# Reordering the last items of a fused token-mixing, attention and int8 kernel, and moving one item to the folded right side

## The chip, the cores and the metric

The kernel runs on one core of a Trainium2 chip. Its time is the device time in microseconds (us) of one execution; the profile's span is the part of it between the first and the last recorded instruction.

## The reference

Four batch rows of 512 image tokens are mixed from `x`, 77 text tokens are appended to each, and two residual blocks follow:

```python
h = einsum('bhid,oi,od->bho', x, weighted_sum, weight)      # 4 x 512 x 256
h = concatenate([h, txt], axis=1)                           # 4 x 589 x 256
h = h + attn(layernorm(h))     # gate * U * cumsum(V) @ out_w + 3-tap convolution along the tokens
n = layernorm(h)
lhs_scale = absmax(n, per row) / 127;   rhs_scale = absmax(rhs, per column) / 127
h = h + (round(n / lhs_scale) @ round(rhs / rhs_scale)) * lhs_scale * rhs_scale
```

## The kernel before

**Tiling.** The tokens of the image are worked in eight *groups* of 256 (two per batch row). The second half of the work goes by twelve *items*, three per batch row: items 0, 3, 6, 9 and 1, 4, 7, 10 are the two blocks of 256 image tokens, items 2, 5, 8, 11 the 77 text tokens. A block of 256 tokens lies as two tiles of 128 partitions by 256 columns, so most steps on it are two instructions and those on a text item are one.

**Stages of an item.** PE adds the convolution (`local`, L1000) and the gated product (`mix`, L1021) to the item's PSUM bank. DVE takes the statistics (`stats`, L717 and L720). POOL works out the reciprocal root (`rstd`, L409). ACT centres the rows (`centre`, L645) and copies them as the residual (`keep`, L653). DVE takes the maximum of each row and its reciprocal (`scale`, L828 and L830). POOL rounds to int16 (`round`, L484) and works out the row's scale (`lscale`, L476). PE transposes (`q_turn`, L1041), ACT turns the integers back into numbers (`ints`, L629), PE multiplies by the right side (`ffn`, L1062 or L1067), DVE scales the product (`out`, L863 or L853), and SP stores the result (L388).

**Two forms of the last steps.** For items below `FIN_ON_DVE` the right side is bf16 integers (`qrhs`, L1062: four matmuls for an item of 256 tokens). DVE then writes the scaled product to `tmp` (L863), and POOL adds the residual into `fin` (L496). For the items from `FIN_ON_DVE` on, the right side has its column scales folded in and is split into two fp32r parts (`srhs_high` of L535, `srhs_low` of L781; L1067: eight matmuls for 256 tokens, four for a text item), and DVE adds the residual itself, into `fin` (L853). The copy of the integers (L629) goes to `qT` in one case and to `qT_wide` in the other.

**Two accumulators.** From item 7 (`ACC_TWO`) on, the products alternate between `uvg_ps` (items 7, 9, 11) and `acc_ps` (items 8, 10). A product waits until the output of the item two before it has been read (L1053 to L1057): product 8 for item 6's output, product 9 for item 7's, product 10 for item 8's, product 11 for item 9's.

**What sets the order.** Each engine runs its own list in strict order. The lists are written out by hand as places: `GROUP_AT` and `ITEM_AT` (L27, L55) give each stage of each group or item a number, and every engine steps through the places and issues what is due. At one place a fixed order of stages holds. For the end of the program the lists before are:

- PE: transpose 8 (1032), convolution 11, product 7 (1034), mix 11 (1035), transpose 9 (1036), product 8 (1037), seven filler matmuls (`WARM_AT`, 1038), transpose 10 (1039), product 9 (1040), product 10 (1041), transpose 11 (1042), product 11 (1043).
- DVE: statistics 10 (73), output 6 (74), scale 10 (75), output 7 (76), statistics 11 (77), output 8 (78), scale 11 (79), outputs 9, 10, 11 (80 to 82).
- POOL: rounding 10 (66), add 7 (67), rounding 11 (68), row scale 10 (69), reciprocal root 11 (70), row scale 11 (71), with the add of item 6 (65) ahead of them.
- ACT: copy 8 (95), keep 8, centre 10 (97), keep 9 (98), copy 9 (99), keep 10 (100), centre 11 (101), copy 10 (102), copy 11 (103), keep 11 (104).

The fillers (`keep_warm`, L1072) multiply a tile of ones into `xt_ps`, which nothing reads afterwards. Another four stand at the start of the program (L1077).

Of the kernel before, what the change touches and what calls it, by code (L numbers as in the profile page):

```python
# [5 lines left out]
P = 128  # L6
# [21 lines left out]
    stats=(2, 6, 13, 23, 31, 40, 50, 57),  # L28
    rstd=(0, 4, 8, 15, 21, 32, 41, 44),
# [26 lines left out]
    put=(-1, -1, 33, -1, -1, 57, -1, -1, 82, -1, -1, 94),  # L56
    conv=(449, 450, 593, 721, 723, 817, 1011, 1015, 1021, 1026, 1028, 1033),
    mix=(451, 465, 594, 722, 724, 818, 1012, 1016, 1024, 1027, 1030, 1035),
    stats=(20, 21, 29, 38, 39, 45, 58, 63, 65, 69, 73, 77),
    rstd=(12, 27, 29, 31, 36, 37, 48, 51, 56, 58, 64, 70),  # L60
    centre=(28, 30, 39, 52, 54, 62, 77, 86, 90, 91, 97, 101),
    keep=(29, 31, 40, 53, 55, 65, 81, 92, 96, 98, 100, 104),
    scale=(24, 25, 34, 42, 43, 48, 61, 66, 70, 72, 75, 79),
    round=(16, 17, 25, 34, 39, 46, 49, 54, 61, 62, 66, 68),
    lscale=(19, 28, 38, 43, 45, 53, 57, 59, 60, 63, 69, 71),
    turn=(609, 641, 753, 898, 1010, 1018, 1025, 1029, 1032, 1036, 1039, 1042),
    ints=(41, 51, 64, 70, 74, 80, 87, 93, 95, 99, 102, 103),
    product=(643, 754, 945, 1013, 1019, 1022, 1031, 1034, 1037, 1040, 1041, 1043),
    out=(33, 41, 53, 59, 62, 68, 74, 76, 78, 80, 81, 82),
    fin=(24, 33, 42, 47, 50, 55, 65, 67),  # L70
)

TXT_AT = dict(turn=337, hidden=354, gates=369, stats=4, uv=12, norm=10, move=13, relu=16, sigmoid=18, rstd=2)
RHS_AT = dict(turn=370, low=0, round=11, out=14, fold=22, fold_low=55, high=0, fold_high=63)
DIAG_AT = 3
WARM_AT = {1038: 7}

FIN_ON_DVE = 8
ACC_TWO = 7
PLAIN = 1  # L80
BY_DMA = 3
# [5 lines left out]
def early_fusion_kernel(nc, x0, x, ws, wt, txt, par, rhs, out, B, HI, T, D, ND, GH, R):  # L87
# [8 lines left out]
    GROUPS = B * HALVES  # L96
# [15 lines left out]
    def item(j):  # L112
        b, i = divmod(j, ITEMS_PER_B)
        return b, i, (2 if i < HALVES else 1), (P if i < HALVES else T)
# [7 lines left out]
    def groups(place, stage):  # L122
        return [g for g, at in enumerate(GROUP_AT[stage]) if at == place]

    def items(place, stage):
        return [j for j, at in enumerate(ITEM_AT[stage]) if at == place]
# [6 lines left out]
    with ExitStack() as ctx:  # L133
        def sb(name, shape, dt=F32):
            return ctx.enter_context(nc.sbuf_tensor(name, shape, dt))

        def sem(name):
            return ctx.enter_context(nc.semaphore(name))
# [50 lines left out]
        lscale = sb("lscale", [P, ITEMS, 2])  # L189
# [6 lines left out]
        fin = sb("fin", [P, 4, 2, D])  # L196
# [14 lines left out]
        def bank(name):  # L211
            return ctx.enter_context(nc.psum_tensor(name, [P, 512], F32))

        h_ps = [bank(f"h_ps{n}") for n in range(4)]
        xt_ps = bank("xt_ps")
# [22 lines left out]
        def wait_fin(eng, j):  # L238

            if j < FIN_ON_DVE:  # L240
                eng.wait_ge(fin_pool, j + 1)
            else:
                eng.wait_ge(fin_dve, j - FIN_ON_DVE + 1)

# [81 lines left out]
        xnT_ready = sem("xnT_ready")  # L326
# [67 lines left out]
        def _(pool):  # L394
# [53 lines left out]
            for place in range(PLACES):  # L448
# [40 lines left out]
                for j in items(place, "fin"):  # L489
                    if j < FIN_ON_DVE:  # L490
                        _, _, nt, rows = item(j)
# [9 lines left out]
        def _(act):  # L501
# [91 lines left out]
            for place in range(PLACES):  # L593
# [29 lines left out]
                for j in items(place, "ints"):  # L623
                    _, _, nt, rows = item(j)
                    act.wait_ge(qt_done, j + 1)
                    if j >= 2:
                        act.wait_ge(acc_done, j - 1)
                    dst = qT if j < FIN_ON_DVE else qT_wide
                    nc.scalar.activation(dst[:, j % 2, :, 0:nt * rows], q16_v[:, :, 0:nt * rows].bitcast(I16),  # L629
# [55 lines left out]
        def _(dve):  # L685
# [117 lines left out]
            for place in range(PLACES):  # L803
# [41 lines left out]
                for j in items(place, "out"):  # L845
                    _, _, nt, rows = item(j)
                    dve.wait_ge(lscale_ready, j + 1)
                    dve.wait_ge(acc_done, j + 1)
                    if j >= FIN_ON_DVE:
                        dve.wait_ge(h2_ready, j + 1)  # L850
# [44 lines left out]
        def _(pe):  # L895
# [36 lines left out]
            def txt_turn():  # L932
                pe.wait_ge(ident_ready, 1)
                pe.wait_ge(txt_normed, 1)
                for c, ps in enumerate((acc_ps, qt_ps)):
                    for b in range(B):
                        last = nc.tensor.transpose(ps[:, b * T:(b + 1) * T], xn_txt[:, b, c * P:(c + 1) * P],
                                                   ident[0:T, 0:T])
                last.then_inc(txt_turned, 1)

            def txt_hidden():
                pe.wait_ge(txt_xnT, 2)
                pe.wait_ge(us_ready, 1)
                pe.wait_ge(hid_ready, 1)
                for c in range(CB):
                    last = nc.tensor.matmul(uvg_ps[:, 0:TB].rearrange("p (b t) -> p b t", b=B), wcat[:, c, :],
                                            xnT[:, c, :, 1 + HI:1 + L], start=(c == 0), stop=(c == CB - 1))
                last.then_inc(txt_uvg, 1)

            def txt_gates():  # L950
                pe.wait_ge(txt_hid, 1)
                nc.tensor.matmul(uvg_ps[0:R, 0:TB], w2[0:GH, 0:R], hid_txt[:, :], start=True, stop=True).then_inc(txt_gate_ps, 1)

            def rhs_turn():
                pe.wait_ge(rhs_rounded, 1)
                pe.wait_ge(txt_xnT, 2)
                for ci in range(CB):
                    for co in range(CB):
                        nc.tensor.transpose(qt_v[:, ci, co * P:(co + 1) * P], vr[:, co, ci * P:(ci + 1) * P],
                                            ident[:, :])  # L960
                for co in range(CB):
                    last = nc.tensor.transpose(acc_ps[:, co * P:(co + 1) * P],
                                               rscale[:, co:co + 1].broadcast_to([P, P]), ident[:, :])
                last.then_inc(rhs_turned, 1)

            def turn(g):
                pe.wait_ge(xn_ready, g + 1)
                if g >= 1:
                    pe.wait_ge(xnT_ready, g)
                    pe.wait_ge(gate_ready, g // HALVES)  # L970
                for c in range(CB):
                    for t in range(2):
                        last = nc.tensor.transpose(xt_v[:, c, t * P:(t + 1) * P],
                                                   xn[:, g % 2, t, c * P:(c + 1) * P], ident[:, :])
                last.then_inc(xt_done, 1)

            def hidden(g):
                b, half = divmod(g, HALVES)
                pe.wait_ge(xnT_ready, g + 1)
                if g == 0:  # L980
                    pe.wait_ge(par_loaded, 16)
                else:
                    pe.wait_ge(us_ready, g)
                    pe.wait_ge(hid_ready, g)
                if g == 1:
                    pe.wait_ge(txt_uv, 1)
                    pe.wait_ge(txt_gate, 1)
                for c in range(CB):
                    last = nc.tensor.matmul(uvg_ps[:, 0:PAIR], wcat[:, c, :],  # L989
                                            xnT[:, c, b, 1 + half * PAIR:1 + (half + 1) * PAIR],  # L990
                                            start=(c == 0), stop=(c == CB - 1))
                last.then_inc(uvg_done, 1)
# [53 lines left out]
            def ffn(j):  # L1046
# [5 lines left out]
                elif j >= 1:  # L1052
                    read = j - 1 if j > ACC_TWO else j  # L1053
                    if read > FIN_ON_DVE:
                        pe.wait_ge(fin_dve, read - FIN_ON_DVE)
# [16 lines left out]
            def keep_warm(out_ap, n):  # L1072
                for _ in range(n):
                    nc.tensor.matmul(out_ap, ones[:, 0:P], ones[:, 0:P], start=True, stop=True)
# [11 lines left out]
            for place in range(PLACES):  # L1086
                step, after = divmod(place, STEP)
                if after == 0 and step < KC * GROUPS:
                    tok(*divmod(step, KC))
                if place in WARM_AT:  # L1090
                    pe.wait_ge(xnT_ready, GROUPS)
                    keep_warm(xt_ps[:, 0:P], WARM_AT[place])
                if place == TXT_AT["turn"]:
                    txt_turn()
                if place == TXT_AT["hidden"]:
                    txt_hidden()
                if place == TXT_AT["gates"]:
                    txt_gates()
                if place == RHS_AT["turn"]:
                    rhs_turn()  # L1100
                for g in groups(place, "turn"):
                    turn(g)
                for g in groups(place, "hidden"):
                    hidden(g)
                for g in groups(place, "gates"):
                    gates(g)
                for j in items(place, "product"):
                    ffn(j)
                for j in items(place, "turn"):
                    q_turn(j)  # L1110
                for j in items(place, "conv"):
                    local(j)
                for j in items(place, "mix"):
                    mix(j)
# [46 lines left out]
```

## Time and profile before

| | us |
|---|---|
| median of 3 runs | 100.16 |
| lowest and highest | 99.6, 100.43 |
| the profiled execution | 99.86 |
| its span | 98.1 |

| engine | busy us | share of the span |
|---|---|---|
| PE (matmul) | 90.9 | 93% |
| DVE | 82.1 | 84% |
| ACT | 75.7 | 77% |
| POOL | 59.9 | 61% |

A busy PE is a modelled figure: matmuls are pipelined, each is recorded from its start to its modelled end, and two that follow each other overlap in the record. In the timelines a row has its start, its length, engine, line, operation, out<-in with its shape and count, and in brackets the idle time before it and who ended that. A time in the rows counts from the span's start. Each fp32 matmul of the fillers leaves two records.

### The profile page before, as it was taken

Reading aid. Unit: us, or ns where it says so; the run is one execution under the profiler, and the core shown is the slowest. Engines: PE = TensorE matmul, PEld = TensorE weight load, DVE = VectorE, ACT = ScalarE, POOL = GpSimd, SP = SyncE. Lnnn points to the kernel's source line nnn. Section 1 sums busy time; section 2 is a strip of 40 time slices with the busy share of each in tenths; the row PEclk is TensorE's granted clock in tenths of the full one; section 3 lists DMA queues with packets and bytes.
Section 4 is the critical chain, followed back from the end, with each engine's and each line's share of the span. In section 5 each row is a group of like instructions: output and inputs, shape, how many; then the busy total and the mean of one; then the engine's idle time right before and its main releaser. Section 6 shows DMA issues by size and latency. Waiting matters only on the chain.

```text
span 98.1 us, 2095 instructions
## 1 busy us (share of the span) xinstructions
PE 90.9 (93%) x682; PEld 82.5 (84%) x682; DVE 82.1 (84%) x217; ACT 75.7 (77%) x151; POOL 59.9 (61%) x105
## 2 busy tenths in 40 slices
PE   5999999999999999699999899999999799999960
PEld 5888889999759998699998789999999568879950
DVE  4196795899489989996989999899999999899680
ACT  1417569979998999968899799587589999898520
POOL 2000033595383757982679899950965896999930
PEclk9999999999999999999999999999999999999999
DMA  1999995089999999999897999792000033010364
GB/s 53 288 289 373 307 258 195 8 247 373 269 184 207 314 257 207 189 277 321 174 301 175 221 211 182 187 168 57 0 20 13 0 110 107 7 36 0 107 226 159
DMA packets 8137, 17.35 MB, mean 177 GB/s; under 512 B 855, under 2 KB 4799, under 8 KB 8127
## 3 DMA queue, kind: packets, MB, share of 16 engines
q0 software_dynamic: 2880, 10.49, 46.1%
q1 hardware_dynamic: 4815, 6.47, 20.9%
q10 hardware_dynamic: 432, 0.27, 0.9%
q8 instruction: 5, 0.08, 0.3%
q14 instruction: 5, 0.04, 0.2%
HBM read 14.81 MB, written 2.41 MB: 176 GB/s over the span
## 4 chain that ended last, share of the span: by engine, by line
PE 34%; ACT 18%; DVE 17%; DMA 13%; POOL 5%; issue 5%; SPq 4%; DVEq 0%; POOLq 0%; ACTq 0%
DMA x_sb<-x_dram 13%; DVE convT L798 8%; PE h_ps L1018 5%; PE h_ps L923 4%; PE uvg_ps L989 4%; ACT x_low L541 4%; PE h_ps L927 4%; PE h_ps L925 4%; SPq L360 4%; PE h_ps L1014 3%; ACT convT L590 2%; ACT tmp L548 2%; ACT xn L636 2%; DVE stats L717 2%; POOL rstd L409 2%
## 5 line engine op out<-in xcount | busy, mean ns | idle before, releaser
L923 PE MATMUL h_ps<-w_high,x_high 128*128 128x256 f32 x112 | 33.7, 301 | 0.9 <-ACT x_sb L653 0.7
L927 PE MATMUL h_ps<-w_high,x_low 128*128 128x256 f32 x112 | 31.3, 280 | 0.0
L925 PE MATMUL h_ps<-w_low,x_high 128*128 128x256 f32 x112 | 31.3, 279 | 0.0
L409 POOL TENSOR_TENSOR rstd<-mv,exponent 128x2 f32<-128x2 f32 (+2 forms) x21 | 17.9, 868 | 16.4 <-DVE mv L720 16.1
L923 PEld LDWEIGHTS h_ps<-w_high,x_high 128*128 128x128 f32 x112 | 21.1, 188 | 2.3 <-issue 2.0
L925 PEld LDWEIGHTS h_ps<-w_low,x_high 128*128 128x128 f32 x112 | 21.1, 189 | 0.2
L927 PEld LDWEIGHTS h_ps<-w_high,x_low 128*128 128x128 f32 x112 | 21.1, 188 | 0.0
L798 DVE SCALAR_TENSOR_TENSOR convT<-xnT,conv_minus,convT 128x255 f32<-128x255 f32 (+1 forms) x24 | 15.4, 695 | 0.1
L717 DVE BATCH_NORM_STATS2 stats<-h_ps 128x6 f32<-128x256 f32 (+1 forms) x36 | 13.8, 420 | 1.8 <-PE h_ps L1027 1.1
L445 POOL DMA_DIRECT2D x_low<-x_dram x10 | 9.7, 969 | 4.5 <-ACT x_low L541 4.5
L484 POOL TENSOR_SCALAR v<-xc,qmul 128x256 int16<-128x256 f32 (+1 forms) x20 | 10.6, 542 | 0.8 <-DVE qmul L830 0.7
L541 ACT ACTIVATE x_low<-x_high 128x1024 fp32r<-128x1024 f32 x10 | 10.6, 1060 | 0.1
L496 POOL TENSOR_TENSOR fin<-tmp,x_sb 128x512 f32<-128x512 f32 (+1 forms) x8 | 9.7, 1207 | 0.6 <-DVE tmp L863 0.6
L645 ACT ACTIVATE xc<-h_ps,mv 128x256 f32<-128x256 f32 (+1 forms) x20 | 8.6, 473 | 1.6 <-DVE mv L720 1.6
L440 POOL DMA_DIRECT2D x_high<-x_dram x10 | 5.9, 608 | 5.7 <-PE h_ps L927 2.9
L590 ACT ACTIVATE convT<-xnT,par_sb,conv_minus 128x255 f32<-128x255 f32 (+1 forms) x16 | 9.3, 633 | 0.1
L989 PE MATMUL uvg_ps<-xnT,par_sb 128*128 128x256 f32 x32 | 8.4, 384 | 0.6 <-ACT xnT L597 0.4
L636 ACT ACTIVATE xn<-h_ps,coef 128x256 f32<-128x256 f32 x16 | 8.1, 559 | 0.5 <-POOL coef L414 0.4
L1014 PE MATMUL h_ps<-ident,convT 128*128 128x128 f32 (+1 forms) x40 | 7.5, 277 | 0.9 <-DVE convT L798 0.6
L620 ACT ACTIVATE glob<-glob 32x256 fp32r<-32x256 f32 (+1 forms) x16 | 7.2, 448 | 1.3 <-POOL glob L425 1.0
L907 PE MATMUL h_ps<-w_tok,x_sb 128*128 128x256 f32 x32 | 7.4, 389 | 0.0
L828 DVE TENSOR_REDUCE amax<-xc 128x2 f32<-128x514 f32 (+1 forms) x12 | 7.0, 582 | 0.3 <-ACT xc L645 0.2
(121 smaller groups left out, 189.9 us busy)
## 6 DMA issues: line engine op xcount, KB each, us to landing
x_high<-x_dram POOLq DMA_DIRECT2D x10, 512.0 KB, 5.1
x_low<-x_dram POOLq DMA_DIRECT2D x10, 512.0 KB, 7.3
x_sb<-x_dram SPq DMA_DIRECT2D x4, 512.0 KB, 9.9
out_dram<-fin SPq DMA_DIRECT2D x8, 256.0 KB
x_sb<-x_dram SPq DMA_DIRECT2D x3, 256.0 KB, 4.3
par_sb<-par_dram SPq DMA_DIRECT2D x1, 325.0 KB, 9.7
txt_sb<-txt_dram SPq DMA_DIRECT2D x1, 308.0 KB
out_dram<-fin SPq DMA_DIRECT2D x4, 77.0 KB
```

Of the source, the lines that this page charges most:

```text
L409: nc.gpsimd.tensor_tensor(out_ap, var_ap, exponent[0:out_ap.shape[0], 0:out_ap.shape[1]], ALU.pow).then_inc(done, 1)
L484: last = nc.gpsimd.tensor_scalar(v[0:rows, j % 2, t, :], xc[0:rows, j % 4, t, 0:D], qmul[0:rows, j, t:t + 1], INT8_MAX, ALU.mult, ALU.mult)
L541: nc.scalar.activation(x_low[:, g % RING, HALF_KC[n], :], x_high[:, g % RING, HALF_KC[n], :], ACT.Copy, scale=-1.0).then_inc(negated[n], 1)
L590: nc.scalar.activation(convT[:, b % 2, c, lo:hi], xnT[:, c, b, 1 + lo:1 + hi], ACT.Identity, scale=conv[:, c, 1:2], bias=outb[:, c:c + 1]) ...
L636: last = nc.scalar.activation(xn[:, g % 2, t, :], h_of(g)[:, t, :], ACT.Identity, scale=coef1[:, 2 * g + t, 1:2], bias=coef1[:, 2 * g + t, ...
L717: last = nc.vector.bn_stats(stats[0:rows, t, 0:6], src(t))
L798: nc.vector.scalar_tensor_tensor(out=convT[:, b % 2, c, lo:hi], in0=xnT[:, c, b, lo + tap:hi + tap], scalar=conv[:, c, tap:tap + 1], in1=c ...
L923: nc.tensor.matmul(h_of(g)[:, t, :], x_high[:, g % RING, kc, at], w_high[:, kc, :], start=(kc == 0 and t == 0), stop=False, skip_group_che ...
L925: nc.tensor.matmul(h_of(g)[:, t, :], x_high[:, g % RING, kc, at], w_low[:, kc, :], start=False, stop=False, skip_group_check=True)
L927: last = nc.tensor.matmul(h_of(g)[:, t, :], x_low[:, g % RING, kc, at], w_high[:, kc, :], start=False, stop=(kc == KC - 1), skip_group_che ...
L989: last = nc.tensor.matmul(uvg_ps[:, 0:PAIR], wcat[:, c, :], xnT[:, c, b, 1 + half * PAIR:1 + (half + 1) * PAIR], start=(c == 0), stop=(c = ...
L1014: nc.tensor.matmul(part, convT[:, b % 2, c, at:at + rows], ident[:, :], start=False, stop=False, is_transpose=True, skip_group_check=True)
```

## The change

Item 7 goes over to the folded right side (`FIN_ON_DVE` from 8 to 7), so its POOL add is gone and `fin` has seven places. On PE product 9 goes from place 1040 to 1038, ahead of transpose 10 (1039), and the seven fillers at 1038 are taken out with the code that issued them. On DVE the order becomes statistics 11 (76), output 7 (77), scale 11 (78), output 8 (79). On POOL it becomes rounding 10 (66), row scale 10 (67), reciprocal root 11 (68), rounding 11 (69), row scale 11 (70). ACT's list stays as it is; its copy of item 7 writes `qT_wide`. The waits follow from `FIN_ON_DVE`: product 9 waits for the first count of `fin_dve`, which item 7's output now gives.

```diff
-    stats=(20, 21, 29, 38, 39, 45, 58, 63, 65, 69, 73, 77),
-    rstd=(12, 27, 29, 31, 36, 37, 48, 51, 56, 58, 64, 70),
+    stats=(20, 21, 29, 38, 39, 45, 58, 63, 65, 69, 73, 76),
+    rstd=(12, 27, 29, 31, 36, 37, 48, 51, 56, 58, 64, 68),
...
-    scale=(24, 25, 34, 42, 43, 48, 61, 66, 70, 72, 75, 79),
-    round=(16, 17, 25, 34, 39, 46, 49, 54, 61, 62, 66, 68),
-    lscale=(19, 28, 38, 43, 45, 53, 57, 59, 60, 63, 69, 71),
+    scale=(24, 25, 34, 42, 43, 48, 61, 66, 70, 72, 75, 78),
+    round=(16, 17, 25, 34, 39, 46, 49, 54, 61, 62, 66, 69),
+    lscale=(19, 28, 38, 43, 45, 53, 57, 59, 60, 63, 67, 70),
...
-    product=(643, 754, 945, 1013, 1019, 1022, 1031, 1034, 1037, 1040, 1041, 1043),
-    out=(33, 41, 53, 59, 62, 68, 74, 76, 78, 80, 81, 82),
-    fin=(24, 33, 42, 47, 50, 55, 65, 67),
+    product=(643, 754, 945, 1013, 1019, 1022, 1031, 1034, 1037, 1038, 1041, 1043),
+    out=(33, 41, 53, 59, 62, 68, 74, 77, 79, 80, 81, 82),
+    fin=(24, 33, 42, 47, 50, 55, 65),
...
-WARM_AT = {1038: 7}
-
-FIN_ON_DVE = 8
+
+FIN_ON_DVE = 7
...
-                if place in WARM_AT:
-                    pe.wait_ge(xnT_ready, GROUPS)
-                    keep_warm(xt_ps[:, 0:P], WARM_AT[place])
```

## Rows read from the trace of the kernel before

**Rows 1.** The page, part 4: shares of the chain that ended last, by engine

```profile
PE 34%; ACT 18%; DVE 17%; DMA 13%; POOL 5%; issue 5%; SPq 4%; DVEq 0%; POOLq 0%; ACTq 0%
```

**Rows 2.** That chain in order of time: start us, length us, what (xcount)

```profile
71.89 1.12 DVE srhs_low L781
...
89.02 0.44 PE uvg_ps L1062 x4
89.46 0.12 PE h_ps L1027
...
90.30 1.56 PE xt_ps L1074 x14
91.86 0.22 PE qt_ps L1041 x4
92.08 1.01 PE uvg_ps L1067 x8
93.09 0.96 PE acc_ps L1067 x8
94.05 0.10 PE qt_ps L1041 x2
...
94.53 0.71 PE uvg_ps L1067 x4
```

**Rows 3.** Timeline of DVE: outputs 7, 8, 9, 11, statistics 11, scale 11

```profile
89.96 0.88 DVE L863 SCALAR_TENSOR_TENSOR tmp<-uvg_ps,lscale,rs_row 128x256 f32<-128x256 f32 x2
90.75 0.42 DVE L717 BATCH_NORM_STATS2 stats<-h_ps 77x6 f32<-77x256 f32 x1
...
91.38 0.48 DVE L853 SCALAR_TENSOR_TENSOR fin<-acc_ps,lscale,x_sb 77x256 f32<-77x256 f32 x1
91.94 0.42 DVE L828 TENSOR_REDUCE amax<-xc 77x1 f32<-77x257 f32 x1
...
93.19 0.88 DVE L853 SCALAR_TENSOR_TENSOR fin<-uvg_ps,lscale,x_sb 128x256 f32<-128x256 f32 x2 [0.64 <-PE uvg_ps L1067]
...
95.31 0.48 DVE L853 SCALAR_TENSOR_TENSOR fin<-uvg_ps,lscale,x_sb 77x256 f32<-77x256 f32 x1 [0.30 <-PE uvg_ps L1067]
```

**Rows 4.** Timeline of ACT: copies 9, 10, 11, keep 10, centring 11

```profile
89.85 0.60 ACT L629 ACTIVATE qT_wide<-qt_ps 128x512 fp32r<-128x512 int16 x1 [0.27 <-PE qt_ps L1041]
90.46 0.60 ACT L653 ACTIVATE x_sb<-h_ps 128x512 f32<-128x512 f32 x1
91.43 0.47 ACT L645 ACTIVATE xc<-h_ps,mv 77x256 f32<-77x256 f32 x1 [0.38 <-DVE mv L720]
92.12 0.60 ACT L629 ACTIVATE qT_wide<-qt_ps 128x512 fp32r<-128x512 int16 x1 [0.21 <-PE qt_ps L1041]
94.17 0.30 ACT L629 ACTIVATE qT_wide<-qt_ps 128x154 fp32r<-128x154 int16 x1 [1.45 <-PE qt_ps L1041]
```

**Rows 5.** Timeline of POOL: rounding 10, add 7, rounding 11

```profile
90.34 0.94 POOL L484 TENSOR_SCALAR v<-xc,qmul 128x256 int16<-128x256 f32 x2
91.24 1.28 POOL L496 TENSOR_TENSOR fin<-tmp,x_sb 128x512 f32<-128x512 f32 x1
92.65 0.47 POOL L484 TENSOR_SCALAR v<-xc,qmul 77x256 int16<-77x256 f32 x1
```

**Rows 6.** Timeline of PE: the transpose of item 10

```profile
91.69 0.39 PE L1041 MATMUL qt_ps<-ident,v 128*128 128x128 bf16 x4
```

**Rows 7.** Stretches: busy us (xcount) of PE, PEld, DVE, ACT, POOL; granted clock; DMA; GB/s

```profile
95.00:95.25 0.25, 0.22 (x2) 0.00 (x0) 0.01 (x1) 0.00 (x0) 0.00 (x0) 1.00 0.94 324
...
96.00:96.50 0.50, 0.00 (x0) 0.00 (x0) 0.00 (x0) 0.00 (x0) 0.00 (x0) 1.00 1.02 346
...
97.00:97.20 0.20, 0.00 (x0) 0.00 (x0) 0.00 (x0) 0.00 (x0) 0.00 (x0) 1.00 0.36 118
...
97.70:98.10 0.40, 0.00 (x0) 0.00 (x0) 0.00 (x0) 0.00 (x0) 0.00 (x0) 0.55 0.00 0
```

**Rows 8.** The page, part 6: the issues of stores, count and size of each

```profile
out_dram<-fin SPq DMA_DIRECT2D x8, 256.0 KB
...
out_dram<-fin SPq DMA_DIRECT2D x4, 77.0 KB
```

## The prediction

> **What bounds the kernel now.** I read the page first. Of the chain that ended last, PE holds the largest share, but only a third [rows 1], so the whole span gives no price for an edit that lies in the last ten microseconds. I therefore read the chain in order of time for that stretch, then the timelines of PE, DVE, ACT and POOL beside it, because the change only permutes waits among these four.
>
> In the chain the reader is to see that PE never waits between item 7's product at 89.02 and item 11's transpose at 94.05: product, mix, product, the seven filler matmuls, transpose, products of items 9 and 10, transpose [rows 2]. Only the last piece leaves PE: ACT turns item 11's integers (94.17 plus 0.31), PE multiplies them (94.53, 0.71), and DVE writes the last result at 95.31 plus 0.48 [rows 2 to 4]. The span ends at 98.1, so 2.3 us of store and shutdown follow.
>
> Two further points of the before order matter. First, the fillers run from 90.30 to 91.86 in the chain's terms [rows 2]; item 10's int16 block, for which the next transpose waits, was finished by POOL at 90.34 + 0.94 = 91.28 [rows 5]. So the fillers hold item 10's transpose (91.69, [rows 6]) by at most about 0.36 us; most of their 1.56 us fills a wait. Second, the order "transpose 10, product 9, product 10" hides ACT's copy of item 10 (92.12 to 92.72, [rows 4]) completely under product 9 (92.08 to 93.09, [rows 2]).
>
> **The change part by part.**
>
> *Item 7 by the folded right side.* Its product has eight fp32r matmuls in place of four bf16 ones. Four bf16 take 0.44 in the chain (89.02), eight fp32r take 0.96 (93.09) [rows 2]: +0.52 us on PE, ahead of mix 11. Its end moves from 89.46 to 89.98, and mix 11's, 0.12 later, from 89.58 to 90.10. The split right side is ready at 71.89 + 1.12 [rows 2], 16 us earlier: no wait. DVE's two output instructions cost the same in either form, 0.88 for two (89.96 against 93.19) [rows 3]. ACT's copy to fp32r is as long as the others of that shape, 0.60 [rows 4]: nothing. POOL loses its add, 1.28 us at 91.24 [rows 5]. What stood behind it, item 11's rounding at 92.65, waits for DVE's scale anyway (91.94 + 0.42, then the reciprocal) [rows 3, 5], and was over at 93.12, nearly a microsecond ahead of the transpose that needs it (94.05): gain zero, and a slip of 0.9 us would be covered too. The store of item 7 on SP leaves when DVE is done and not POOL; item 8's store stands behind it. Neither is the last, so they count nothing.
>
> *Item 11's statistics before item 7's output on DVE.* DVE is free at about 90.0 (it began item 7's output at 89.96) [rows 3]. In the new order it must first see mix 11. From a product's end to DVE's first read 0.10 us pass (92.08 + 1.01 = 93.09 against 93.19) [rows 2, 3]. So the statistics start at 90.20 instead of 90.75. They occupy 0.63 (90.75 to the next instruction at 91.38) [rows 3]; item 7's output starts at 90.83 instead of 89.96 and ends at 90.83 + 0.88 = 91.71. Behind it stand item 11's scale and item 8's output.
> Does the earlier statistic help? The next user is ACT's centring of item 11, but ACT goes through its own list first: item 9's copy, item 10's keep, then the centring [rows 4]. Item 9's transpose slips with PE by the 0.52, so ACT's copy runs from 89.85 + 0.52 = 90.37 to 90.97 and the keep to 91.58 (0.60 each), and the centring starts at about 91.6 where it started at 91.43. The early statistics buy nothing; ACT takes them in.
>
> *Product 9 ahead of transpose 10, no fillers.* Product 9 writes the bank that item 7's output reads, so it waits for that output: 91.71. PE's transposes of item 10 and all else stand behind it. This is the step that decides. The wait before was covered: item 7's output ended by about 90.8, a microsecond before product 9 at 91.89. The restart after a wait is priced by product 11: 0.06 from ACT's end (94.17 + 0.30 = 94.47) to PE at 94.53, then 0.71 for four matmuls [rows 2, 4]; four more at 0.96/8 = 0.12 make 1.19 for eight. In a row, from the output of item 7:
> product 9 runs 91.77 to 92.96; transpose 10 adds 0.22 [rows 2], 93.18; ACT follows by 0.04 and takes 0.60 [rows 4], 93.82, and PE now waits, since nothing is left to put between; product 10 runs 93.88 to 95.07; transpose 11 adds 0.10 [rows 2], 95.17; ACT's copy, 0.02 later and 0.30 long, ends at 95.49; product 11 runs 95.55 to 96.26; the last output starts 0.07 later, at 96.33. Before, it started at 95.31 [rows 3]. Sum: +1.02 us.
> Split up: product 9's end moves from 93.09 to 92.96 (-0.13); the exposed transpose and copy of item 10 and the restart add 0.22 + 0.04 + 0.60 + 0.06 = 0.92; product 10 costs 1.19 for 0.96 (+0.23). -0.13 + 0.92 + 0.23 = 1.02.
>
> *The end.* Stores move at 346 GB/s in their densest stretch [rows 7], which makes the 256 KB before the last store about 0.77 us. The gap between the outputs of items 10 and 11 stays near what it was (product 10 to product 11 still has one transpose, one copy and one restart in it), so the last 2.3 us stay. If item 9's store delayed the later ones, its leaving earlier relative to them gives something back: the last three stores hold 589 KB [rows 8], 1.7 us at that rate, in the 2.2 us from 95.0 to 97.2 [rows 7], so the queue had slack and I count nothing; 0.2 is kept for the low end.
>
> **The number.** The profiled execution took 99.86 us with a span of 98.1; with +1.02 it is 100.88. The median of the three runs stands 0.30 above the profiled one, 100.16, so I predict 101.2.
>
> *Bounds of this sum.* Low: mix 11 might finish early enough that DVE is never idle (statistics at 90.0, -0.20) and both restarted products might cost a stream's 0.96 rather than 1.19 (-0.46), or the 0.2 of the stores: not all at once, I take +0.6. High: the product at 1.01 rather than 0.96 three times (+0.15, the first row of rows 2 for eight is 1.01) and waits for DVE at 0.10 rather than 0.06: +1.25.
>
> **The rivals.**
>
> A, the forecast: item 7's output holds product 9, and item 10's copy stands bare. +0.6 to +1.25, 100.8 to 101.4. Chance 0.70.
>
> B, not slower by what can be told: product 9 isn't held by item 7's output, but only by its own operand, ACT's copy of item 9, which ends at 90.97 in the new order. It decides if item 7's output ends before that, so starts before 90.09; then product 9 starts at 91.03 and everything after is 0.74 earlier than in A: +0.28, 100.4. For it: DVE is idle from 90.0, the gap to be made up is small. Against: the statistics alone fill 0.63 of it, and they stand first in DVE's list. Chance 0.12.
>
> C, the clock: PE now stands from 90.82 (product 8 ended at 90.30, plus 0.52) to 91.8 and from 93.2 to 93.9, at the place where the fillers were. The profile's granted clock is full through all of this kernel's work and falls only at the end: in 97.70 to 98.10 it is 0.55 on average, so it fell at about 97.74, with PE idle since 95.24 [rows 2, 7]. That idle stretch was 2.5 us long, more than twice either gap here, which speaks against a fall. If it fell all the same (from 2.4 to 1.2 GHz), each 256-column matmul would take about 0.24 for 0.12; with products 10 and 11, twelve of them, that is +1.4 on top of A: 102.6. Chance 0.10. The Trainium skill (TensorE: Matmul & The Clock Gate, "What's actually happening") says that the clock is throttled by default and given for activity, and its section on the PE-mode transpose adds that transposes don't count as PE being busy in the same way. By that the fillers were worth something and the transposes left in the gap are not; if it bit here, the time would be C's. No row of before shows PE at the lower clock with work to do.
>
> D, faster: PE's work bounds the stretch, and the change takes 1.56 of fillers and adds 0.52, so 1.04 less. Even then item 10's block is not there before 91.28, so a transpose could come 0.36 earlier at most: 99.8; the unlimited form gives 99.1, and that is what this rival stands for. It would need the exposed copy of item 10 to vanish, and nothing in the order lets it. Chance 0.05.
> The remaining 0.03 is for something that none of these names, either way.
>
> **Chances.** About 1% is what a measurement of this kernel can tell from no change, here 1.0 us. A's centre lies on that line: a little over half of A, 0.37, is beyond it. C adds 0.10 and the unnamed 0.01 to slower: 0.48. B, A's other part (0.33) and 0.01 of the unnamed make 0.46 for the same; D and the last 0.01 of the unnamed leave 0.06 for faster by over 1%. The range 100.3 to 101.9 leaves out D, most of C, the unnamed and the tail of B, some 0.2 in all. A by itself is 100.8 to 101.4.
>
> **What the profile of the changed kernel would show.** Right: item 7's output on DVE starting after the 77-row statistics, at 90.8; PE waiting before product 9 for DVE (0.8 us or so) and again before product 10 for ACT's copy (0.65 or so); the last output at 96.3 and the span at 99.1. Item 11's centring on ACT no earlier than before. POOL's item 7 add gone, with no wait shortened on the chain. Wrong in size: product 9 released by ACT's copy rather than DVE (B); a granted clock under 1.00 in the stretch from 91 to 96 (C); transpose 10 ending before 92.1 (D). The prediction would be wrong altogether if the part of the program before 88 us moved, where no instruction is changed.

## The result, and the profile after

| | before | changed |
|---|---|---|
| median | 99.84 us (22 executions, 99.27 to 103.44) | 100.64 us (22 executions, 99.39 to 103.36) |
| ratio to before | 1 | 1.0091, 95% interval 1.006 to 1.0122 |
| profiled execution | 99.86, span 98.1 | 100.62, span 98.8 |

The changed kernel is 0.9% slower: 0.91 us by the ratio, between 0.6 and 1.2. The whole of it is in the last ten microseconds. Before that the two executions differ by chance: mix 9 begins at 83.52 in the changed kernel and at 83.76 before, though no instruction ahead of it was touched; the executions of the kernel before alone lie further apart than that (99.27 to 103.44 us). So the two ends are set against each other from a point that both share: DVE's maximum of item 10 (`amax`, the first part of scale 10). It begins at 89.13 before and at 88.89 after. From there to the last output it is 95.31 - 89.13 = 6.18 us before [rows 3] and 96.11 - 88.89 = 7.22 us after: +1.04. Below, this stretch is called the *tail*. The ratios leave out the executions that took over 1.5% longer than the fastest of their kernel, so they are not the quotients of the medians; the profiled executions of f3, f4, g2 and a1 below are among those left out, and of them only the tail is used.

The chain of the changed kernel in order of time, from the product of item 7 (start us, length us, what):

```profile
88.79 0.95 PE uvg_ps L1066 x8
89.74 0.12 PE h_ps L1026
89.86 0.25 PE qt_ps L1040 x4
90.11 0.02 issue
90.14 0.61 ACT qT_wide L628
90.74 0.77 issue
91.52 1.18 PE uvg_ps L1066 x8
92.70 0.26 PE qt_ps L1040 x4
92.95 0.02 issue
92.98 0.61 ACT qT_wide L628
93.58 0.04 issue
93.63 1.21 PE acc_ps L1066 x8
94.84 0.10 PE qt_ps L1040 x2
94.94 0.02 issue
94.97 0.31 ACT qT_wide L628
95.28 0.04 issue
95.32 0.71 PE uvg_ps L1066 x4
```

These are the lines that answer to [rows 2]. Where the chain of before stayed on PE from 89.02 to 94.05, it now leaves PE twice more. Once it does so before product 9 (91.52), where 0.77 us of "issue" stands between ACT's copy of item 9 and the product, and once before product 10 (93.63), where ACT's copy of item 10 lies bare. What the 0.77 us is, the chain doesn't say. DVE's timeline of the same kernel does:

```profile
88.89 0.69 DVE L827 TENSOR_REDUCE amax<-xc 128x2 f32<-128x514 f32 x1 [0.16 <-ACT xc L644]
...
89.89 0.43 DVE L716 BATCH_NORM_STATS2 stats<-h_ps 77x6 f32<-77x256 f32 x1
90.36 0.19 DVE L719 BATCH_NORM_AGGREGATE mv<-stats 77x2 f32<-77x9 f32 x1
90.54 0.88 DVE L852 SCALAR_TENSOR_TENSOR fin<-uvg_ps,lscale,x_sb 128x256 f32<-128x256 f32 x2
91.61 0.42 DVE L827 TENSOR_REDUCE amax<-xc 77x1 f32<-77x257 f32 x1 [0.20 <-ACT xc L644]
...
92.24 0.48 DVE L852 SCALAR_TENSOR_TENSOR fin<-acc_ps,lscale,x_sb 77x256 f32<-77x256 f32 x1
...
96.11 0.48 DVE L852 SCALAR_TENSOR_TENSOR fin<-uvg_ps,lscale,x_sb 77x256 f32<-77x256 f32 x1 [0.30 <-PE uvg_ps L1066]
```

Item 7's output ends at 90.54 + 0.88 = 91.42, and product 9 begins 0.10 later. ACT's copy, to which the profile's list of waits puts the wait down (0.9 us), had been over since 90.74. It is the case in which a wait with several conditions is ascribed to the wrong one.

Two stretches of the changed kernel, PE's two waits (busy us and count for PE, PEld, DVE, ACT, POOL; granted clock; DMA; GB/s):

```profile
90.58:91.52 0.94, 0.01 (x2) 0.04 (x1) 0.83 (x2) 0.94 (x3) 0.94 (x4) 1.00 0.50 170
92.94:93.63 0.69, 0.00 (x1) 0.00 (x1) 0.69 (x2) 0.60 (x1) 0.01 (x1) 1.00 0.33 104
```

PE stands for 0.94 and 0.69 us, at the full clock.

### The profile page after: what moved, and what is told of

It reads as the page before. It is cut to its first block, busy times and chain, and to the rows that moved or that the text cites. A ratio compares the mean times of both kernels' runs of the same rounds, so it can differ in the third digit from the quotient of the medians.

```text
span 98.8 us, 2075 instructions
## 1 busy us (share of the span) xinstructions
PE 89.8 (91%) x672; PEld 81.5 (82%) x672; DVE 82.1 (83%) x217; ACT 75.4 (76%) x151; POOL 59.7 (60%) x104
## 4 chain that ended last, share of the span: by engine, by line
PE 28%; DVE 21%; ACT 19%; DMA 12%; issue 7%; POOL 6%; SPq 5%; DVEq 0%; POOLq 0%; ACTq 0%
DMA x_sb<-x_dram 12%; DVE convT L797 8%; PE h_ps L1017 4%; ACT x_low L540 4%; SPq L359 3%; PE uvg_ps L988 3%; PE h_ps L922 3%; PE uvg_ps L1066 3%; PE h_ps L1013 3%; DVE stats L716 3%; PE h_ps L926 3%; PE h_ps L924 3%; ACT convT L589 2%; ACT tmp L547 2%; DVE tmp L862 2%
## 5 line engine op out<-in xcount | busy, mean ns | idle before, releaser
L483 POOL TENSOR_SCALAR v<-xc,qmul 128x256 int16<-128x256 f32 (+1 forms) x20 | 11.2, 588 | 1.3 <-DVE qmul L829 1.3
L495 POOL TENSOR_TENSOR fin<-tmp,x_sb 128x512 f32<-128x512 f32 (+1 forms) x7 | 8.4, 1201 | 0.6 <-DVE tmp L862 0.6
```

The lines of the kernel that those rows point to most:

```text
L483: last = nc.gpsimd.tensor_scalar(v[0:rows, j % 2, t, :], xc[0:rows, j % 4, t, 0:D], qmul[0:rows, j, t:t + 1], INT8_MAX, ALU.mult, ALU.mult)
```

## The experiments

Theory H is the prediction's: product 9 is held by item 7's output, and item 10's copy then lies bare. Its rivals have their letters in the expectations. Every kernel was timed beside the kernel before. A tail is read from one profiled execution. Measured tails and ratios together:

| kernel | what it is | tail us | against 6.18 | ratio (95% interval) |
|---|---|---|---|---|
| changed | | 7.22 | +1.04 | 1.0091 (1.006 to 1.0122) |
| e1 | DVE: output 7 ahead of statistics 11 | 6.58 | +0.40 | 1.0068 (1.0038 to 1.0097) |
| e2 | PE: transpose 10 ahead of product 9 | 6.36 | +0.18 | 0.9993 (0.9952 to 1.0033) |
| e3 | both | 6.56 | +0.38 | 1.0026 (0.9987 to 1.0065) |
| f1 | e3, output 8 ahead of scale 11 | 5.89 | -0.29 | 0.9945 (0.9901 to 0.999) |
| f3 | changed, output 8 ahead of scale 11 | 7.20 | +1.02 | 1.0046 (0.9987 to 1.0104) |
| e4 | before without fillers | 5.83 | -0.35 | 0.9936 (0.9897 to 0.9975) |
| f4 | before with four fillers | 5.83 | -0.35 | 0.9967 (0.9923 to 1.0011) |
| f2 | f1, rounding 10 ahead of add 6 | 7.68 | +1.50 | 1.0128 (1.005 to 1.0207) |
| g1 | f2, keep 10 after copy 10 | 6.43 | +0.25 | 1.0102 (1.0039 to 1.0165) |
| g2 | f2 with five fillers | 7.23 | +1.05 | 1.0104 (1.0059 to 1.0149) |
| g3 | changed with seven fillers | 7.21 | +1.03 | 1.0083 (1.0036 to 1.013) |
| a1 | the changed kernel again | 8.32 in its trace | | 1.0081 (1.0038 to 1.0124) |

The ratios tell apart what differs by some 0.5%. Smaller steps are read from the tails.

**e1: item 7's output first again.**

```diff
-    stats=(..., 73, 76),
+    stats=(..., 73, 77),
-    out=(..., 74, 77, 79, 80, 81, 82),
+    out=(..., 74, 76, 79, 80, 81, 82),
```

> The changed kernel with one thing undone: DVE takes item 7's output ahead of item 11's statistics again (places 76 and 77), PE's order stays changed. Theory H (product 9 is held by item 7's output, then item 10's copy stands bare): in the changed kernel's trace product 7 ends at 89.74 and DVE's idle begins at about 89.7, so the output would run 89.85 to 90.73 instead of 90.54 to 91.42, and product 9 would start at about 90.82 (ACT's copy of item 9 ends at 90.74) instead of 91.52. All after it comes 0.7 us earlier: about +0.3 us against the kernel before, ratio 1.003, and item 10's bare copy stays, with PE waiting about 0.7 us before product 10. Rival W (product 9 is released by ACT's copy of item 9, as the profile's wait list says, and the DVE order costs nothing): no change against the changed kernel, ratio 1.009. Rival S (item 11's later statistics become the bound: statistics at 90.7, scale 11 at 92.0 to 92.6, rounding to 93.1): the transpose of item 11 would wait, and less than 0.3 us would come back.

Product 9 started at 90.95, 0.09 after item 7's output (89.98 + 0.88 = 90.86). That is 1.91 after item 10's maximum began, where the changed kernel needs 2.63: 0.72 earlier. The tail is 0.64 shorter. H expected 0.7, rival W nothing. Rival S doesn't show: the rounding of item 11 ended at 93.14, a microsecond ahead of its transpose. 0.08 went elsewhere, and the trace shows where. Product 10 started at 93.16, 0.10 after item 8's output (92.58 + 0.48), while ACT's copy was over at 93.02. That second hold by DVE mattered more in e3. By the ratio alone e1 would not be told from the changed kernel.

**e2: transpose 10 first again.**

```diff
-    product=(..., 1034, 1037, 1038, 1041, 1043),
+    product=(..., 1034, 1037, 1040, 1041, 1043),
```

> The changed kernel with one thing undone: on PE product 9 goes back behind item 10's transpose (place 1040), without fillers; DVE's order stays changed. Theory H: product 9 still waits for item 7's output (start 91.52 in the changed kernel's times), but item 10's transpose has gone ahead in the gap at about 91.1 and ACT's copy lies under product 9. Product 10 follows product 9 in a stream: products 9 and 10 end at about 92.7 and 93.7 instead of 92.7 and 94.84. About 1.15 us come back: ratio to the kernel before about 0.999 (0.1 us faster). Rival K (the fillers' absence costs something by itself, a lower granted clock or a slower restart after idle): the ratio stays over 1.004 and the matmuls of products 9 and 10 lie more than 0.13 us apart. Rival W: no change, 1.009.

The ratio, 0.9993, is the expected one: the loss of the changed kernel is gone, as far as an interval of 0.4% either way can tell. The tail gave back 0.86 where 1.15 was expected. The missing 0.29 is the hold that e1 had shown: item 8's output ends at 91.55 + 0.48 = 92.03 and product 10 begins at 92.13, after a wait of 0.12, so that it takes 1.18 in the chain and not the 0.96 to 1.02 of a stream. Rival W falls. So does K: the matmuls of a product are 0.12 apart as before.

**e3: both undone.**

```diff
-    stats=(..., 73, 76),
+    stats=(..., 73, 77),
-    out=(..., 74, 77, 79, 80, 81, 82),
+    out=(..., 74, 76, 79, 80, 81, 82),
-    product=(..., 1034, 1037, 1038, 1041, 1043),
+    product=(..., 1034, 1037, 1040, 1041, 1043),
```

> The changed kernel with both orders undone: DVE takes item 7's output first and PE transposes item 10 ahead of product 9; what is left of the change is item 7 on the folded right side, no fillers, and POOL's list. Theory H, with the two costs independent where both lie on the chain: item 10's transpose at 91.1 (POOL's rounding of item 10 ends at 91.05 in the changed kernel's times), product 9 behind it at 91.3 with no wait, product 10 ending at 93.3. Against the kernel before, whose fillers hold the transpose until 91.69 in its own times, 0.35 us faster: ratio 0.9965. Item 11's rounding then ends at about 93.1, just ahead of its transpose. Rival S (item 11 becomes the bound): no faster than e2, ratio 0.999 or above, and PE waits for POOL before item 11's transpose. Rival K: ratio over 1.002 with a granted clock under 1.00 between 90 and 96.

This missed. The tail is 6.56, 0.2 longer than e2's and 0.7 longer than H allowed, though every wait that H names is gone. Its chain in order of time, from POOL's rounding of item 10:

```profile
89.17 0.95 POOL v L483 x2
90.12 0.05 issue
90.17 0.40 PE qt_ps L1040 x4
90.57 1.00 PE uvg_ps L1066 x8
91.57 0.50 issue
92.07 1.18 PE acc_ps L1066 x8
```

Product 9 follows the transpose without a wait, as expected. Then 0.50 us of "issue" stand before product 10, and again no copy of ACT ends there. DVE's timeline of e3 has item 8's output, the reader of the bank that product 10 writes:

```profile
90.86 0.42 DVE L827 TENSOR_REDUCE amax<-xc 77x1 f32<-77x257 f32 x1 [0.54 <-ACT xc L644]
91.31 0.16 DVE L829 RECIPROCAL qmul<-amax 77x1 f32<-77x1 f32 x1
91.48 0.48 DVE L852 SCALAR_TENSOR_TENSOR fin<-acc_ps,lscale,x_sb 77x256 f32<-77x256 f32 x1
```

It ended at 91.96, 0.11 before product 10. The change had put item 8's output behind item 11's scale as well, and that scale stood for 0.54 us for ACT's centring. Rival S is refuted in its form (PE does not wait for POOL before transpose 11), but its remark that item 11's chain gets in the way was nearer the mark than H. It also says why e3, with one delay fewer, is slower than e2: with item 7's output first, the statistics and the centring of item 11 come later, and item 8's output ends 4.00 us after item 10's maximum begins (e2: 3.81). The new theory, H2: product 10 waits for item 8's output, and this hold was hidden in the changed kernel behind the bare copy.

**f1: item 8's output first.** It has e3's lists, but for these two:

```diff
-    scale=(..., 75, 78),
-    out=(..., 74, 76, 79, 80, 81, 82),
+    scale=(..., 75, 79),
+    out=(..., 74, 76, 78, 80, 81, 82),
```

> Item 7 on the folded right side and no fillers, with the orders of PE and DVE as in the kernel before; POOL's list as in the changed kernel. It differs from e3 in one point: DVE writes item 8's output ahead of item 11's scale. Theory H2 (the e3 kernel lost what it should have gained because product 10 waits for item 8's output, 0.50 us of PE idle ending 0.11 after that output): the output comes at about 90.3 in e3's times, product 10 follows product 9 in a stream, and from item 10's maximum on DVE to the last output it is 5.85 us, as in e4 (6.56 in e3, 6.18 before): ratio 0.9965, 0.3 to 0.4 us faster. Rival F (the folded item 7 costs something by itself, its 0.5 us on PE or ACT): ratio 0.999 or above, and from the maximum to the last output 6.2 us or more, with PE not waiting before product 10.

The 0.50 us are gone. Products 9 and 10 follow each other (90.65 plus 1.01, 91.66 plus 1.02 in the chain), the tail is 5.89, and the ratio is 0.9945, below one by its interval. H2 holds. So does the claim that the folded item 7 is free once nothing waits for it: against e4, which has the bf16 form and the POOL list of before, the tail is 0.06 longer, and product 10 is 0.06 longer too (1.02 for 0.96).

**f3: the same step in the changed kernel.** The diff is f1's, with item 7's output at 77 as in the changed kernel.

> The changed kernel with only this moved: DVE writes item 8's output ahead of item 11's scale. Theory H (in the changed kernel product 10 is held by ACT's bare copy of item 10, which ends 0.9 us after item 8's output, so the output has slack): no change against the changed kernel: ratio 1.009, from item 10's maximum to the last output 7.2 us. Rival O (item 8's output holds product 10 here as it does in e3): 0.4 us come back, ratio 1.005, 6.8 us.

The tail is 7.20, no change: item 8's output has 0.9 us of slack there, as H2 says. The ratio, 1.0046, has an interval that holds both expectations, so it settles nothing.

**e4 and f4: the fillers.**

```diff
-WARM_AT = {1038: 7}
+WARM_AT = {}          (f4: {1038: 4})
```

> The kernel before with the seven fillers taken out and nothing else. Theory H (fillers fill a wait and overrun it by up to 0.36 us): item 10's transpose starts when POOL has rounded item 10 (91.3 instead of 91.69), all later steps follow: 0.3 to 0.4 us faster, ratio 0.9965, with PE idle for about a microsecond before the transpose. Rival K (the idle microsecond costs clock): the granted clock falls under 1.00 between 91 and 96 and the twenty 256-column matmuls of products 9 to 11 slow from 0.12 us apart, up to 2.4 us: ratio 1.01 to 1.02. Rival N: the transpose isn't bound by the fillers, ratio 1.000.

> The kernel before with four fillers instead of seven. One filler takes 0.22 us (1.56 for seven), so they end about 0.67 us sooner than seven, at 91.19 in the times of before, where POOL's rounding of item 10 ends at 91.28. Theory H (fillers cost only what they overrun the wait by): the same as none at all, 0.35 us faster than before, ratio 0.9965 or as e4's 0.9936 within the intervals; from item 10's maximum to the last output 5.85 us. Rival K (what fillers do to the clock or the restart is worth having): clearly faster than e4. Rival L (each filler costs its own 0.22 us): half-way between before and e4, 6.03 us.

Both tails are 5.83, 0.35 shorter than before, and transpose 10 starts when POOL has rounded item 10: in e4 at 90.48, after 89.50 + 0.94 = 90.44. The fillers of before cost what they overran the wait by, 0.35 us. Rival L (each costs its own 0.22) would have given 6.03. In e4 PE stood for 1.04 us without a loss of clock in any of its 12 executions (no mean clock below 0.999).

**f2, g1, g2: the next step, which fails.** With the fillers gone the chain runs through POOL's rounding of item 10, which begins 0.3 us late behind an add. f2 turns the two round.

```diff
-    round=(..., 66, 69),      fin=(..., 55, 65),
+    round=(..., 66, 67),      fin=(..., 55, 66),
-    rstd=(..., 64, 68),       lscale=(..., 63, 67, 70),
+    rstd=(..., 64, 69),       lscale=(..., 63, 68, 70),
```

> f1 with POOL's list changed: rounding 10 ahead of item 6's add, and rounding 11 ahead of row scale 10 and reciprocal root 11. In e3 and e4 POOL's rounding of item 10 starts about 0.3 us after DVE has the scale (89.50 against 89.17 in e4), since item 6's add (1.29 us) stands ahead of it. Theory H (the chain runs through that rounding to item 10's transpose once the fillers are gone): rounding, transpose and all after it come about 0.3 us earlier than in f1: ratio 0.993 to 0.994, from item 10's maximum to the last output about 5.55 us. Rival P (the chain is elsewhere, or item 11's rounding becomes late): no gain over f1, ratio 0.9965, and PE waits for POOL before item 11's transpose.

It missed, and by far. The rounding starts at once, but the tail is 7.68. ACT's timeline of f2, keep 10, centring 11 and copy 10:

```profile
92.70 0.60 ACT L652 ACTIVATE x_sb<-h_ps 128x512 f32<-128x512 f32 x1 [1.44 <-POOL fin L495]
93.19 0.46 ACT L644 ACTIVATE xc<-h_ps,mv 77x256 f32<-77x256 f32 x1
93.55 0.59 ACT L628 ACTIVATE qT_wide<-qt_ps 128x512 fp32r<-128x512 int16 x1
```

Item 10's keep writes the buffer that item 6's add reads. The add came 1.9 us later (it begins 1.89 us after item 10's maximum, and in f1 0.05 before it), and ACT's whole list stood for it: 1.44 us. The expectation had counted only who waits for the rounding. It had not asked who waits for the add.

g1 moves the keep behind the copy:

```diff
-    keep=(..., 98, 100, 104),
+    keep=(..., 98, 102, 104),
```

> f2 with one thing moved: ACT keeps item 10 after its copy of item 10 instead of before item 11's centring. In f2 ACT stood for 1.44 us before that keep, since the keep reuses the buffer that POOL's add of item 6 reads, and that add had been put behind the rounding; centring 11, copy 10 and product 10 stood behind it. Theory A (that wait is the whole of f2's loss): the 1.4 us come back. ACT's centring of item 11 then waits for DVE's statistics and ends about 2.9 us after item 10's maximum began on DVE, copy 10 ends 0.5 later, and product 10 starts about where it does in f1: from the maximum to the last output 6.0 us (f2 7.68, f1 5.89), ratio 0.996. The rounding that comes 0.3 us earlier buys nothing, because ACT's list then holds product 10. Rival: the earlier rounding does pay once the keep is out of the way: 5.6 us, ratio 0.992. Rival: something else was slow in f2: over 6.5 us.

Product 10 starts 3.42 us after item 10's maximum, as it does in f1 (3.44): so far as expected, and the earlier rounding buys nothing. But the tail is 6.43 and not 6.0. Its chain shows what the late add holds next:

```profile
91.07 1.25 POOL fin L495
92.32 0.02 issue
92.34 2.17 DMA out_dram<-fin
...
94.63 0.09 DVE fin L852
```

Item 6's store now ends at 94.51, and item 10's output writes the same slot of `fin`. Product 11 was done at 94.27 + 0.71 = 94.98, but its output, last in DVE's list behind item 10's, started at 95.58; 0.1 us after the product, as elsewhere, would have made the tail 5.9. g1's ratio, 1.0102, is higher than a tail of +0.25 explains; some 0.13 more lies behind the last output (98.5 - 95.58 = 2.92, against 2.79 before), and the rest of it stays open within its interval, which is wide (six executions).

g2 fills the gap before product 10 in f2:

```diff
+WARM_AT = {1041: 5}
```

> f2 with five fillers between product 9 and product 10, in the gap where PE stood for 1.38 us. In f2 the granted clock fell to half while product 11 ran, its four matmuls 0.22 us apart for 0.12. Theory C (it is the long wait of PE before product 10 that lowers the clock): with the gap filled the clock stays 1.00 to the last product, product 11 is 0.45 us shorter and from item 10's maximum to the last output it is 7.2 us for 7.68; executions with a mean clock near 0.98 are gone; the ratio is 1.005 to 1.010 for f2's 1.0128. Rival N (the fall has nothing to do with the gap): clock and 7.68 us as in f2.

The reason for it is the clock in f2. Stretches of f2, columns as above:

```profile
92.00:94.00 2.00, 0.81 (x7) 0.60 (x6) 0.58 (x2) 1.30 (x3) 0.61 (x1) 1.00 0.23 74
94.00:95.00 1.00, 0.81 (x6) 0.81 (x7) 0.95 (x4) 0.14 (x1) 0.60 (x3) 1.00 1.03 346
...
95.50:96.00 0.50, 0.12 (x1) 0.12 (x2) 0.50 (x2) 0.47 (x2) 0.23 (x2) 0.78 0.07 21
96.00:97.00 1.00, 1.00 (x4) 0.64 (x4) 0.37 (x1) 0.09 (x1) 0.00 (x0) 0.50 0.77 262
```

PE stood for 1.38 us before product 10, and at about 95.8 the clock fell to 1.2 GHz, after product 10 had already run. Product 11's four matmuls took 1.15 us in the chain for 0.71. With the fillers (g2) the clock is full until PE has finished, product 11 takes 0.71, and the tail is 7.23. That is what theory C expects. Of the 1.79 us by which f2's tail is longer than f1's, 0.45 is thus the clock and 1.34 the waits. That the fillers kept the clock up is supported and not shown: mean clocks near 0.98 were seen in two of f2's six executions and in none of g2's twelve, and if the fall were as likely with fillers as without, both cases would still land among f2's six about one time in ten.

**g3 and a1: fillers in the changed kernel.**

```diff
+WARM_AT = {1038: 4, 1041: 3}
```

> The changed kernel with fillers put back where PE now stands: four before product 9 (0.89 us in a gap of 0.93) and three before product 10 (0.67 in 0.69). Theory H (the gaps of the changed kernel cost no clock and the fillers end before the wait does): the same time as the changed kernel beside it, from item 10's maximum to the last output 7.2 us. Rival C (the absence of fillers is part of the changed kernel's loss): faster than the changed kernel by 0.3 us or more. Rival R (a product that follows fillers restarts faster than one that follows idle time, 0.96 for 1.19 us): up to 0.4 us faster.

> The changed kernel itself, on the same chip and beside the same runs as g1 to g3, so that they can be set against it: ratio 1.009, from item 10's maximum to the last output 7.22 us.

g3's tail is 7.21 and its ratio 1.0083, beside 1.0081 for the changed kernel timed with it. The missing fillers are no part of the usual loss, and rival R falls too: product 9 takes 1.19 us after fillers as after idle time. The fillers don't hold the products either, as theory H has it: product 9 begins 0.10 after item 7's output (89.19 + 0.88 = 90.07, and 90.17), 2.62 us after item 10's maximum for 2.63 in the changed kernel, and product 10 4.73 after it for 4.74.

But a1's profiled execution was not the expected one. PE's timeline around product 10, and the stretches:

```profile
93.15 0.38 PE L1066 MATMUL acc_ps<-srhs_high,qT_wide 128*128 128x256 f32 x1 [0.69 <-ACT qT_wide L628]
93.37 0.32 PE L1066 MATMUL acc_ps<-srhs_low,qT_wide 128*128 128x256 f32 x1
93.49 0.41 PE L1066 MATMUL acc_ps<-srhs_high,qT_wide 128*128 128x256 f32 x1
93.70 0.41 PE L1066 MATMUL acc_ps<-srhs_low,qT_wide 128*128 128x256 f32 x1
```

```profile
92.00:93.00 1.00, 0.46 (x6) 0.24 (x5) 0.92 (x3) 0.50 (x1) 0.47 (x2) 1.00 0.65 218
93.00:94.00 1.00, 0.85 (x5) 0.85 (x6) 0.19 (x1) 0.09 (x1) 0.00 (x0) 0.73 0.26 79
94.00:95.00 1.00, 1.00 (x7) 0.84 (x6) 0.00 (x0) 0.00 (x0) 0.00 (x0) 0.50 0.76 262
```

The clock fell at about 93.46, with product 10 under way, and from there the matmuls are 0.21 apart. The tail is 8.32, 1.10 more than in the other execution of the same instructions. So the fall of rival C exists in this kernel, in some executions only: of the 34 executions of the changed kernel, this one had a mean clock of 0.97 and one of the first 22 had 0.983, the longest of all at 103.36 us. The clock explains little of that one: a mean of 0.983 over its span of 101.6 us is 3.5 us at half clock, and if these were its last, only product 11 fell in them (in the changed kernel it begins 98.8 - 95.32 = 3.5 us before the end), an estimate of at most 0.44 us. What made the rest stays open; the kernel before has one of 103.44. Of e1's twelve executions, one had 0.983 too. g3, with fillers, had none below 0.993 in 12. Two in 34 against none in 12 shows no difference by count, so that fillers prevent it rests on f2 against g2 alone and is not shown.

## Why the prediction was right, and where it wasn't

**The sum held.** +1.02 us was forecast for the tail and 1.04 measured. The time was 100.64 for 101.2; over half of the difference is the kernel before, whose median was 99.84 this time and 100.16 in the runs shown. The forecast as a ratio is 1.010, the measured one 1.0091. The prediction took 1% for the least that can be told from no change; the interval came out at 0.3% either way, so that 0.9% is told. The terms, shifted by the 0.24 us by which the changed execution was ahead:

- Product 7 in eight matmuls: 0.96 forecast, 0.95 measured.
- The statistics of item 11: from 90.20, measured 89.89 + 0.24 = 90.13. DVE reads 0.03 after the end of mix 11 and not 0.10.
- The end of item 7's output: 91.71, measured 91.66. Product 9: 91.77, measured 91.76. Here two small errors cancel, since PE starts 0.10 after DVE (the row it was priced by had ACT as the releaser, with 0.06).
- Restarted products 1.18 and 1.21 for 1.19; transpose 10 0.26 for 0.22; ACT's copy 0.60 for 0.60; the rest as forecast.
- The end: from the start of the last output to the end of the span it is 98.8 - 96.11 = 2.69, for 2.79 before. The forecast left it as it was, so 0.1 us came back there. (The 0.77 us for 256 KB at 346 GB/s should be 0.74, or 0.76 with 1024 bytes to the KB; nothing rests on it.)
- ACT takes in the earlier statistics: centring 11 at 91.11 + 0.24 = 91.35, forecast 91.6, before 91.43. Earlier by 0.08, and of no use to the end. The forecast gave copy 9 and keep 10 on ACT 0.60 each; they begin at 90.14 and 90.63, and the centring at 91.11, so the steps are 0.49 and 0.48.
- POOL's shorter list gained nothing; rounding 11 ended 1.9 us ahead of transpose 11.
- The fillers' overrun, at most 0.36: e4 measured 0.35.

**The price of a restart is right, its name is not.** The chain counts a product in a stream only from the end of the record before it. PE's timeline of the kernel before has the first and the last matmul of product 9, in a stream:

```profile
91.89 0.36 PE L1067 MATMUL uvg_ps<-srhs_high,qT_wide 128*128 128x256 f32 x1
...
92.81 0.28 PE L1067 MATMUL uvg_ps<-srhs_low,qT_wide 128*128 128x256 f32 x1
```

From start to end that is 93.09 - 91.89 = 1.20 us, and product 9 of the changed kernel, after its wait, has 92.70 - 91.52 = 1.18. The product is no slower. What the wait takes away is the overlap of its first matmuls with the records before them. Only product 10 is in part slower by itself: 1.12 in the stream (92.93 to 94.05), where its second matmul begins 0.12 after the first, and 1.21 after the wait, where it begins 0.22 after. The wait needn't be the cause of that part: f1's product 10, in a stream, has 0.20 and 1.19 (91.49 to 92.68).

**Rival B** (product 9 held by ACT's copy alone) is refuted by e1, where taking the output first moved product 9 by 0.72. **Rival D** is refuted by the result.

**Rival C: the argument against it fails.** It set PE's gaps of 1.0 and 0.7 us against the 2.5 us of idle time that the clock outlasted at the end of the kernel before, and took the shorter ones for safe. a1 and f2 show the fall after gaps of 0.94 plus 0.69 and of 1.38. One idle stretch is no measure of what a stretch with work in it does. C was given a chance of 0.10 as if it were a property of the kernel; it is one of the execution. Its price depends on when the fall comes: 1.10 us in a1, where two of the twelve matmuls of products 10 and 11 were already out (forecast for all twelve: 1.4), and 0.45 in f2, where only product 11 was left.

**What the prediction did not see** is the third reordering. It named item 8's output as standing behind item 7's and the scale, and gave it no price, rightly for the changed kernel, where the bare copy covers it. It became the bound as soon as that cover was taken away: e1 and e2 give back 0.64 and 0.86 singly, 1.50 in sum, and together 0.66.

So the parts of the change come to this, in the tail: without fillers -0.35 (e4); item 7 on the folded side, with POOL's list, +0.06 (f1 against e4); the orders of DVE and PE +1.33 (the changed kernel against f1), of which no clean share belongs to one.

**Better than both** the kernel before and the changed one are e4 and f1, at 0.9936 and 0.9945. Each has an interval below one, and they aren't told from each other. e4 is the kernel before with the filler line emptied.

## What to carry to other kernels

When an order is changed by hand, ask of each moved instruction not only what it waits for but what it frees: the bank, the residual's buffer, the slot of a store. All four waits that decided here (product 9 on output 7, product 10 on output 8, ACT's keep on an add, an output on a store) came from the reuse of a buffer, and the first two appeared in the profile as "issue" or under another engine's name, so that one has to look for whose end lies 0.1 us ahead. Two delays that hide each other can't be priced by undoing each alone; and a filler is worth only the wait that it covers, so its count should end before the awaited operand comes.

## What the hardware showed that was not expected

- The granted clock can fall while PE is at work, 0.3 us into product 10 in a1, or with work still to do, between products 10 and 11 in f2; the gaps before it were 0.94 and 0.69 us in the one and 1.38 in the other. The same instructions with the same gaps kept the full clock until PE was done in the profiled execution of the changed kernel, and e4 kept it over a gap of 1.04. At 1.2 GHz the 256-column matmuls are 0.21 us apart for 0.12.
- The Trainium skill (TensorE: Matmul & The Clock Gate, "What's actually happening") ties the throttled clock to an idle stretch of PE. f2's and a1's traces agree only in part: PE was idle in pieces, with a product between or behind them, when the clock went. Whether transposes count as work for the clock, which the prediction asked, no run here tells.
- A product of eight after a wait adds 1.18 to 1.22 us to the chain and one in a stream 0.95 to 1.02, though both take 1.12 to 1.22 from start to end: a record of 0.28 us every 0.12 overlaps its neighbour, and a wait ends the overlap. Fillers in the wait don't bring it back (g3: 1.19 and 1.18).
